# Row statistics of the next tile issued one tile ahead, and both hi halves before the lo halves, in the layer-norm stage of a convolution-attention layer

## The reference, cut to what matters

```python
xn = _layernorm(x, axis=-1)                 # x: [2, 4096, 4096] f32
c  = conv1d(xn, conv_w, kernel 3, SAME) + conv_b      # 4096 -> 3*1024 = q, k, v
q, k, v = per-head projections wq, wk, wv             # 16 heads of 64
o  = causal softmax attention inside blocks of 128 rows; o = o @ wo + bo
s  = o @ proj_w + proj_b                              # 1024 -> 4096
logits = xn @ router_weight.T + router_bias           # 64 experts, top 8 of the softmax
g  = silu(xn * sum(top 8 weights) + w_dense @ expert_bias)
out = x + s * g
```

## Time and profile before

| | |
|---|---|
| median of 2 runs | 1894.72 us (1891.86 to 1897.58) |
| the profiled execution, its own time | 1897.37 us |
| its span, core 6, the slowest | 1895.8 us |
| spans of the eight cores | 1864.0 to 1895.8 us |
| mean granted clock of TensorE, core 6 | 0.855 of full speed |
| busy in the span: PE, DVE, ACT, POOL | 1577.0, 393.6, 384.1, 229.3 us |
| bytes moved by DMA | 163.68 MB |

### The profile page before, as it was taken

How to read it: one execution, slowest core, us unless ns; L and a number is a source line. 1 busy time by engine, 2 the same in 40 slices (tenths; PEclk the granted TensorE clock), 3 DMA queues, 4 the chain that set the end, 5 groups by cost and what they waited for, 6 DMA issues and landing times.

```text
span 1895.8 us, 18983 instructions; the slowest of 8 cores (1864.0 to 1895.8 us)
## 1 busy us (share of the span) xinstructions
PE 1577.0 (83%) x7996; PEld 763.2 (40%) x7996; DVE 393.6 (21%) x644; ACT 384.1 (20%) x453; POOL 229.3 (12%) x180
## 2 busy tenths in 40 slices
PE   3356799999999999999999999987757765976772
PEld 3356444444444444444444444333434432322220
DVE  2776100000000000000000000002363251454564
ACT  1443000000000000000000000396354341423322
POOL 0000011111111111111111111000000000142243
PEclk7777899999999999999999999998555556777775
DMA  5997666666666666666666666624000037035334
GB/s 139 227 244 157 78 76 72 75 78 78 78 74 73 76 78 78 76 74 74 77 78 78 76 71 77 100 45 90 1 1 1 0 67 155 12 105 157 93 94 171
DMA packets 230825, 163.68 MB, mean 86 GB/s; under 512 B 74691, under 2 KB 222403, under 8 KB 226499
## 3 DMA queue, kind: packets, MB, share of 16 engines
q0 software_dynamic: 155472, 92.97, 39.0%
q1 hardware_dynamic: 75270, 69.50, 14.2%
HBM read 220.69 MB, written 16.78 MB: 125 GB/s over the span
## 4 chain that ended last, share of the span: by engine, by line
PE 62%; DMA 12%; DVE 9%; ACT 7%; POOL 4%; issue 3%; SPq 3%; POOLq 0%; DVEq 0%; ACTq 0%
PE pCv L644 53%; DMA AL<-x 7%; PE pWO L925 4%; DMA AL<-pw 4%; POOL AL L1061 2%; ACT AL L706 2%; POOL AL L1064 2%; DVE AL L799 1%; PE pQ L728 1%; SPq L426 1%; DVE tStat L330 1%; DVE tRs L791 1%; ACT L706 1%; DVE tSc L777 1%; DVE AL L851 1%
## 5 line engine op out<-in xcount | busy, mean ns | idle before, releaser
L644 PE MATMUL pCv<-AL 128*128 128x512 bf16 x4608 | 1000.6, 379 | 0.0
L644 PEld LDWEIGHTS pCv<-AL 128*128 128x128 bf16 x4608 | 449.5, 98 | 550.7
L777 DVE TENSOR_REDUCE tSc<-pS 128x1 f32<-128x512 f32 x32 | 21.8, 683 | 1190.5 <-PE pS L770 1190.5
L587 POOL DMA_DIRECT2D AL<-cw x144 | 125.9, 875 | 1054.4 <-PE pCv L644 863.7
L659 ACT ACTIVATE AL<-pCv,tCbT 128x512 bf16<-128x512 f32 x48 | 29.1, 688 | 889.2 <-PE pCv L644 889.2
L993 PE MATMUL pPr<-AL 128*128 128x512 bf16 x448 | 122.9, 424 | 21.3 <-DVE AL L1041 21.3
L464 PE MATMUL pLgT<-AL 128*64 128x128 bf16 x768 | 61.5, 260 | 87.6 <-DMA AL<-AL 87.6
L925 PE MATMUL pWO<-AL 64*128 64x256 bf16 x512 | 109.8, 416 | 5.7 <-DVE AL L851 5.7
L464 PEld LDWEIGHTS pLgT<-AL 128*64 128x64 bf16 x768 | 60.4, 139 | 88.8 <-issue 88.8
L925 PEld LDWEIGHTS pWO<-AL 64*128 64x128 bf16 x512 | 74.4, 146 | 40.3 <-issue 6.6
L993 PEld LDWEIGHTS pPr<-AL 128*128 128x128 bf16 x448 | 42.5, 105 | 97.2 <-issue 64.7
(11 more groups left out here) (97 smaller groups left out, 933.6 us busy)
## 6 DMA issues: line engine op xcount, KB each, us to landing
AL<-cw POOLq DMA_DIRECT2D x144, 512.0 KB, 6.0
AL<-x SPq DMA_DIRECT2D x16, 2048.0 KB, 15.6
out<-AL SPq DMA_DIRECT2D x8, 2048.0 KB, 9.5
AL<-pw POOLq DMA_DIRECT2D x8, 1024.0 KB, 8.2
AL<-wq POOLq DMA_DIRECT2D x1, 2048.0 KB, 17.5
AL<-wk POOLq DMA_DIRECT2D x1, 2048.0 KB, 14.8
AL<-wv POOLq DMA_DIRECT2D x1, 2048.0 KB, 15.2
AL<-wo POOLq DMA_DIRECT2D x1, 2048.0 KB, 16.7
```

What stands on the lines that cost most here:

```text
L587: sCWs[gi % 4].add(e.dma_start(out=cwr[:, gi % 4, :].rearrange("p (g f) -> p g f", g=8), in_=d_cw[s, g].rearrange("g p f -> p g f")), 16)
L644: ins = e.matmul(p_cv[:, 512 * (bs + 2 * sub + hf): 512 * (bs + 2 * sub + hf) + 512], lhsT, xnTh[:, o:o + 512], start=(step == 0), stop=(s ...
L777: cNM.add(e.reduce_max(nmax[Q % 2][:], p_S[:, 512 * (Q % 2):512 * (Q % 2) + 512], axis=AX.X, negate=True), 1)
```

## The change

```diff
+        def emit_stats(e, j):
+            xt_ = xslots[j % 2]
+            rows_ = slice(0, 16) if j == NTILE else slice(0, 128)
+            jc_ = 8 if j == NTILE else j
+            wait_xload(e, j)
+            sb0 = 48 * jc_
+            ins = None
+            for c in range(8):
+                ins = e.bn_stats(t_stat[rows_, sb0 + 6 * c:sb0 + 6 * c + 6],
+                                 xt_[rows_, 512 * c:512 * c + 512])
+            dedge(e, ins)
+            cAG.add(e.bn_aggr(t_mrv[rows_, 2 * jc_:2 * jc_ + 2],
+                              t_stat[rows_, sb0:sb0 + 48]), 1)
+
+        @DV
+        def _(e):
+            emit_stats(e, 0)
+
         for j in range(NTILE + 1):
...
-            @DV
-            def _(e, j=j, xt=xt, rows=rows, jc=jc):
-                wait_xload(e, j)
-                sb0 = 48 * jc
-                ins = None
-                for c in range(8):
-                    ins = e.bn_stats(t_stat[rows, sb0 + 6 * c:sb0 + 6 * c + 6],
-                                     xt[rows, 512 * c:512 * c + 512])
-                dedge(e, ins)
-                cAG.add(e.bn_aggr(t_mrv[rows, 2 * jc:2 * jc + 2],
-                                  t_stat[rows, sb0:sb0 + 48]), 1)
...
             @DV
             def _(e, j=j, rows=rows, jc=jc):
+                if j + 1 <= NTILE:
+                    emit_stats(e, j + 1)
                 e.wait_ge(cSQ.h, j + 1)
                 dedge(e, e.reciprocal(t_r[rows, jc:jc + 1], t_sc1[rows, :]))
...
             for h in range(2):
                 @DV
                 def _(e, j=j, h=h, xt=xt):
                     e.wait_ge(cMR.h, j + 2)
...
                     cHI.add(e.tensor_scalar(hiB[:, 2048 * h:2048 * h + 2048],
...
+            for h in range(2):
                 @DV
                 def _(e, j=j, h=h, xt=xt):
                     e.wait_ge(cHI.h, 2 * j + h + 1)
```

## The result

The changed kernel takes 1946.96 us (median of 11 runs, 1938.85 to 1959.15) against 1888.03 us for the kernel before (median of 10, 1877.9 to 1897.58): a ratio of 1.0316, 95% interval 1.0277 to 1.0354, so 58.9 us slower. Forecast were 65.9 us more and 1961 us, with a range of 1946 to 1974. The kernel before ran 6.7 us lower over ten runs than in the two that were known, which is half of the distance between 1961 and 1947; the other half is the 7 us by which the loss was put too high. So the time stands only 1 us inside its range. The loss stands well inside: less the 1894.7 that the forecast added it to, the range is 51 to 79 us more.

A forecast was written before the change was run, and what follows sets the result against it. The first 210 us were taken to have no slack behind them, and a serial load ring to bound them: six turns of 27.0 us and the halo end the stage at 244.9, 65.9 later; 1894.7 + 65.9 gives 1961 us, range 1946 to 1974.

The forecast's parts named there:

- The ring: First stage, per tile: load lands, statistics, hi 0, SP's four issues, next load, all in series; 27.0 us against 17.55.
- Step 1: Load of x for a tile, issue to landing: 10.4 us, with 8.8 as the lower end.
- Step 2: DVE, statistics to the end of hi 0, with the square root's wait gone: 7.4 us.
- Step 3: SP, end of hi 0 through four transpose issues to the next load's issue: 9.2 us.
- The turn: One load's issue to the next in the first stage: 10.4 + 7.4 + 9.2 = 27.0 us, against 17.55 before.
- The halo and the end: End of first stage: halo's load issued at 222.1, landing in 4 us; last router group at 244.9 us.
- The signs: Trace after: DVE waits for x about 13 us, loads 27 us apart, halo's about 222, convolution about 275.
- PE's last group: Last group of router matmuls on PE: a clock difference costed at nothing, 2 us kept either way.
- Hi 1 ahead of lo 0: DVE's order of halves: hi 1 about 3.8 us sooner; without it SP's stretch 3.1 us longer per turn.
- A: Rival: loads stay hidden and the square root's wait goes, 15.9 us; 1879 us, or some 1887; 5%.
- B: Rival: load takes 8.8 us and SP's stretch 7.4, a turn 23.6, total 1941 us; 10%.
- C: Rival: load waits for the transposes to drain, taking 12.6 us, a turn 29.2, total 1974 us; 8%.

The follow-up runs named there:

- e1: Changed kernel with the old order of halves (hi 0, lo 0, hi 1, lo 1), statistics still ahead: 1977.77 us, ratio 1.0433 to the kernel before.
- e6: Changed kernel with the loads of tiles 2 to 7 cut to two rows: turn 20.5 us, convolution start 237.2 us.
- e8: Changed kernel with the loads of tiles 2 to 7 cut to half the columns: turn 23.4 us, convolution start 253.0 us.
- e9: Changed kernel with the load placed between the hi and lo transposes in SP's queue: ratio 1.0166 to the kernel before, turn 21.7 us.
- e11: Kernel before with order hi 0, hi 1, lo 0, next tile's statistics, lo 1, and SP's load between hi and lo transposes: ratio 0.9947.
- e2: Kernel before with only the new order of halves (hi 0, hi 1, lo 0, lo 1), statistics where they were: ratio 0.9967.
- e3: Changed kernel with the loads of x for tiles 2 to 8 issued from POOL's queue: ratio 1.0621 to the kernel before.
- e4: Kernel before with the new order of halves and the loads of x issued from POOL's queue: ratio 0.9992.

## Why the prediction was right

**The ring.** Right, and it is what was measured: with the load's place, its bytes and the order of the halves changed one at a time, the turn moved each time by what was changed (e1, e6, e8, e9).

**Step 1, the load, 10.4 us.** Too high. On core 7 after, six loads took 11.8, 9.0, 8.6, 9.2, 8.2 and 8.8 us from issue to landing, 9.3 us as the mean. 10.4 was the median of three loads of core 6, those whose landing the line view has; the same view gives 9.3 to 10.1 on six of the other cores (core 7: 11.0), and after 8.5 to 9.1 on all eight. The loads of the earlier trace rows had hi transposes issued on their heels. That this speaks for less was said, and the value was kept all the same; no run separates the two. The estimate from the Trainium skill ("DMA: Bandwidth & Descriptors", Bandwidth, and Latency and other measured facts), 7.9 us, lies below all six; the lowest is 8.2. That it would have given 1946 us, next to the 1947 measured, is luck: the loads took longer, and the kernel before had turned out lower.

**Step 2, statistics to hi 0, 7.4 us.** 99.58 to 106.84 is 7.26 with SP's 0.07 in it, against 7.47. Right.

**Step 3, hi 0 to the next load, 9.2 us.** Too low: 9.8, 9.6, 9.4, 10.9, 9.9 and 9.9 us, mean 9.9, counted from SP's start, where the forecast had 9.1. The term that was mis-sized is the pair of hi issues, put at 1.84 and 1.78 us from rows where SP had been idle before each. Right behind one another they take 4.5 us; the lo pair is as forecast. The chain that ended last, core 7 after:

```profile
106.84 2.17 SPq L434
109.11 2.21 SPq L434
111.41 2.45 SPq L439
113.95 2.36 SPq L439
116.47 8.53 DMA AL<-x
```

**The turn, 27.0 us.** 26.5. The errors of steps 1 and 3, -1.1 and +0.8, partly cancel. That the sum came out better than its terms is luck; the ring itself is not.

**The halo and the end.** The halo's load took 3.5 us (4 was taken), issued at 220.6 (222.1). From SP's first hi issue of tile 7, at 231.36, to the router's last group at 243.54 are 12.2 us (11.3). The last group stood at 244.9 in the forecast.

**Where the 65.9 went to 58.9.** As the mean of the eight cores the last router group moved from 180.7 to 240.8, 60.0 us, as it did on core 7 (183.50 to 243.54). Of the 5.9 us between 65.9 and 60.0, 1.7 are the point of reference: the sum was set against core 6 before, which had its last group at 179.03, while the eight cores lay between 177.5 and 183.65. The other 4.1 are the end of the sum, 244.9: on core 6 itself a turn was 26.2 us after, and the halo's load was issued at 217.65 where the sum had 222.1. What is left, from 60.0 to 58.9, is within the interval.

**The range.** 1946 to 1971 does not follow from the terms listed for it. Added plainly they are 20 down and 15 up, 1941 to 1976; by squares 11 down and 7 up, 1950 to 1968, and the measured 1947 would have been outside. That it is inside its range is therefore no evidence of how well the sizes were known; the turn and the waits are.

**The signs.** DVE's waits for x of tiles 2 to 7 on core 7 were 15.3, 12.6, 12.0, 12.4, 12.9 and 12.5 us (13 forecast), the halo's load was issued at 220.6 (222), no wait for the square root was left but the last, and the convolution began at 273.3 (275), with the same lengths behind it.

**The smaller terms.** PE's last group, put at no difference, took 7.49 us against 7.88: right. Hi 1 ahead of lo 0 was costed at 3.1 us a turn saved; e1's turn is 2.0 us longer than after's, and 2.4 by the stretch from statistics to load. Mis-sized for the same reason as step 3.

**Rivals.** A (loads hidden, 1879 to 1887) did not occur, and its condition, a load issued some 10 us before it is asked for, was named rightly: e9, with the load 4.5 us sooner, does not meet it and still has the ring; e11, with the statistics behind lo 0, does, and the ring is gone. Its price was wrong, since 15.9 us of waits gave 10 us at best, and that with the halves' order in it, which alone gave some 6 (e2). The page's rule cited there (the Trainium skill, "Perfetto Trace Analysis", Optimization Strategy) points at a gap that was there, and the gap went; it does not ask what the same move will make DVE wait for, and 16.3 us of waits for x became 100.5. B is in part what happened: the load nearer to 8.8 than to 10.4, but not the cheaper issues. C, a load of 12.6 us, did not occur but perhaps in the first turn, whose load took 11.8 us on core 7 and 8.4 to 12.3 on the eight cores.

## What to carry to other kernels

An engine's queue is in order, so an instruction moved ahead takes its wait with it, and everything behind it inherits that wait; before moving one, ask when the thing it waits for was issued, and whether that issue stands behind the work that is now held up. With two buffers this closes a ring: here the refill of a buffer waited for the very tile that now waited for the refill, and 15.5 us of small waits were traded for 84 us of large ones. And a gap on one engine is worth only what the next bound leaves: without the data of x the reordering of e11 gave 26.5 us, with it 7.6.

## What the runs showed of the hardware that was not expected

In e3, loads of 2 MB from POOL's queue, issued just behind the start of DMA transposes from SP's queue, landed in 10.0 to 10.2 us on cores 0, 2, 4 and 6 and in 24.3 to 26.2 us on cores 1, 3, 5 and 7 (medians by core). In e4 those issued ahead of the transposes landed in 10.0 to 12.5 us on the odd cores too. From ACT's queue, or from SP's own, they took 8 to 12 us on all. The Trainium skill ("DMA: Bandwidth & Descriptors", Issuing engines are not separate DMA queues) has it that issuing from several engines saves only the time of the issue and that the transfers interleave; for SP against ACT the runs agree (a turn of 21.7 and of 21.9 us), for POOL beside transposes on the odd cores of e3 they don't.

The issue of a DMA transpose by SP is no fixed price. Before, it was 1.8 us with SP idle ahead of it, and 7.9 us behind a load in flight. After, in the chain of core 7, the first of four in a row took 1.8 to 2.2 us, the second 2.2 to 2.6, the third and fourth 2.2 to 3.4.
